# The offsets' outer tap columns moved by two SBUF transfers instead of two shifting products, in a deformable convolution stage

## The reference, cut to what matters

```
x = x + deform_conv(ln_c(x))        # layer 0, the stage that the change is in
    # offset  = conv3x3(ln_c(x), w_off)          18 numbers for each pixel
    # sampled = bilinear gather of ln_c(x) at 9 taps moved by the offsets
    # out     = sum over taps and channels of sampled * w_conv
t = t + top2_experts(ln_t(t))       # layer 0, experts
x = x + fourier_mix(ln_c(x))        # layer 1
t = t + routed_ffn(ln_t(t))         # layer 1
```

## Time and profile before

| | |
|---|---|
| median of 3 runs | 3994.7 us (3988.97 to 3998.19) |
| span of the profiled execution, first to last instruction | 3990.2 us |
| PE busy | 3781.9 us, 95% of the span |
| DVE busy | 2579.8 us, 65% |
| ACT busy | 1794.4 us, 45% |
| POOL busy | 1553.5 us, 39% |
| queue q1 (SP's transfers) | 630.17 MB, 57.1% of 16 engines |
| queue q10 (ACT's transfers) | 71.85 MB, 5.8% of 16 engines |

### The profile page before, as it was taken

How to read it: one execution, slowest core, us unless ns; L and a number is a source line. 1 busy time by engine, 2 the same in 40 slices (tenths; PEclk the granted TensorE clock), 3 DMA queues, 4 the chain that set the end, 5 groups by cost and what they waited for, 6 DMA issues and landing times. The chain is left out here.

```text
span 3990.2 us, 88376 instructions
## 1 busy us (share of the span) xinstructions
PE 3781.9 (95%) x31447; PEld 2461.4 (62%) x31447; DVE 2579.8 (65%) x8511; ACT 1794.4 (45%) x4685; POOL 1553.5 (39%) x2661
## 2 busy tenths in 40 slices
PE   6999999999999999999997999999999999997468
PEld 5666666666666666666663566666666666664245
DVE  4444444444444444444426999999999999996633
ACT  4555555555555555555530334344343434344124
POOL 4544545455444544445422333232323233333210
PEclk8999999999999999999997999999999999998755
DMA  6555555555555554555525777777777777885779
GB/s 117 102 97 96 91 93 95 89 101 93 88 97 91 101 92 89 95 91 91 88 47 194 270 276 268 276 269 277 266 278 271 275 271 270 280 300 175 270 292 394
DMA packets 611673, 709.79 MB, mean 178 GB/s; under 512 B 62256, under 2 KB 494256, under 8 KB 594848
## 3 DMA queue, kind: packets, MB, share of 16 engines
q1 hardware_dynamic: 505760, 630.17, 57.1%
q10 hardware_dynamic: 104448, 71.85, 5.8%
q0 software_dynamic: 1024, 2.10, 0.1%
HBM read 521.20 MB, written 181.63 MB: 176 GB/s over the span
## 5 line engine op out<-in xcount | busy, mean ns | idle before, releaser
L366 PE MATMUL a_ob<-a_sr,wcv 128*128 128x512 f32 (+3 forms) x2820 | 1081.6, 518 | 0.8 <-DVE a_xo L496 0.8
L436 ACT COPY a_sr<-a_sb 128x576 f32<-128x576 f32 (+7 forms) x1296 | 621.2, 562 | 903.9 <-PE a_sb L351 895.9
L351 PEld LDWEIGHTS a_sb<-a_tt,a_win 32*128 32x128 f32 x19008 | 655.7, 185 | 264.6 <-issue 247.7
L351 PE MATMUL a_sb<-a_tt,a_win 32*128 32x144 f32 x19008 | 748.6, 300 | 19.2 <-ACT a_sr L436 12.7
L521 POOL TENSOR_TENSOR a_sx<-a_hh 128x576 f32<-128x576 f32 x260 | 377.8, 1453 | 929.9 <-DVE a_hh L473 921.8
L366 PEld LDWEIGHTS a_ob<-a_sr,wcv 128*128 128x128 f32 x2820 | 491.3, 191 | 279.0 <-issue 231.5
L1116 DVE TENSOR_TENSOR b_P<-b_P,b_x 128x1024 f32<-128x1024 f32 x512 | 620.2, 1212 | 1.8 <-DMA b_P<-pd 1.8
L473 DVE TENSOR_SCALAR a_hh<-a_hh 128x576 f32<-128x576 f32 (+1 forms) x128 | 59.5, 465 | 841.0 <-ACT a_hh L415 841.0
L1019 PE MATMUL b_z<-b_P,b_ew 128*128 128x512 f32 x1024 | 463.4, 595 | 0.0
L1022 PE MATMUL b_z<-b_P,b_ew 128*128 128x512 f32 x1024 | 460.3, 592 | 0.0
L1245 POOL TENSOR_TENSOR b_ss<-b_st 128x12 f32<-128x12 f32 (+2 forms) x139 | 30.0, 216 | 1058.1 <-DVE b_pp L1190 963.8
(11 more groups left out here) (186 smaller groups left out, 5302.4 us busy)
## 6 DMA issues: line engine op xcount, KB each, us to landing
b_P<-pd SPq DMA_DIRECT2D x128, 2048.0 KB, 7.6
a_win<-xtp SPq DMA_DIRECT2D x2144, 36.0 KB
a_xin<-in_x SPq DMA_DIRECT2D x128, 256.0 KB, 6.3
xtp<-a_tn ACTq DMA_DIRECT2D x128, 256.0 KB, 2.3
x1d<-a_xo SPq DMA_DIRECT2D x128, 256.0 KB, 5.9
b_x<-x1d SPq DMA_DIRECT2D x128, 256.0 KB, 7.5
x2d<-b_xa SPq DMA_DIRECT2D x128, 256.0 KB, 3.4
pw<-x3d SPq DMA_DIRECT2D x128, 256.0 KB, 6.6
```

What stands on the lines that cost most here:

```text
L351: t = e.matmul(d[:, 0:3 * m_, :, NU_ * i:NU_ * i + NU_], win[32 * q:32 * q + 32, half_of(Q, j) % NWH, NWIN // 3 * h + i, :], m, start=(j = ...
L366: t = e.matmul(ob[:, r:r + m, :], k["wcv"][:, 3 * (2 - kr) + kx, :], rows[:, :, t_, :], start=(t_ == 0 and r == 0), stop=(t_ == 8))
L436: a = e.copy(bass.AP(d.tensor, d.offset, [list(d.ap[0]), [1152, ni], [1536, nk], [32, 4], [1, m]]), bass.AP(v.tensor, v.offset, [list(v.ap ...
```

## The change

The two shifting products and their constant go. In their place SP issues two transfers for each group, from `zz` to a new buffer `zs` in SBUF: column kx = 0 from partitions 0..126 to 1..127, column kx = 2 from 1..127 to 0..126, 72 numbers (288 bytes) for each partition. `zs` is set to zero once, so the edge rows stay zero. `zz` is laid out with the tap column ahead of the row, so that a column is contiguous. DVE adds three operands in two instructions, the second waiting on the first. The PE wait of `conv` half 1 on `on_ready` goes, since the PSUM bank is no longer shared. In the table `offs` moves from slot 2 to 4, `offs_out` from 3 to 5, `reach` from 4 to 5, `place` from 3 to 4, `hats` from 4 to 5 and `bend` from 7 to 8.

```diff
@@ order_a
             put(t0 - 1, "zsum", Z)
             put(t0 + 1, "shift", Z)
-            put(t0 + 2, "offs", Z)
-            put(t0 + 3, "offs_out", Z)
-            put(t0 + 4, "reach", Z)
-            put(t0 + 3, "place", Z)
-            put(t0 + 4, "hats", Z)
-            put(t0 + 7, "bend", Z)
+            put(t0 + 4, "offs", Z)
+            put(t0 + 5, "offs_out", Z)
+            put(t0 + 5, "reach", Z)
+            put(t0 + 4, "place", Z)
+            put(t0 + 5, "hats", Z)
+            put(t0 + 8, "bend", Z)
             put(t0 + 9, "clip", Z)
@@ phase_a, buffers
-    zz = S("a_zz", [128, 2, 4, 3, 18])
+    zz = S("a_zz", [128, 2, 3, 4, 18])
+    zs = S("a_zs", [128, 2, 2, 4, 18])
@@ phase_a, tensor
-                if h:
-
-                    w.wait_ge(on_ready, min(G - 2, NG - 1) + 1)
-            elif o[0] == "shift":
-                G = o[1]
-                w.wait_ge(z_step, z_count[G])
-
-                w.wait_ge(on_ready, G)
-                w.wait_ge(y_ready, 4 * min(G + 2, NG))
-
-                for kx in (0, 2):
-                    t = e.matmul(OF[:, :, :], k["shift"][:, kx, :], zz[:, G % 2, :, kx, :], start=(kx == 0),
-                                 stop=(kx == 2))
-                t.then_inc(shifted, 1)
@@ phase_a, vector
-                w.wait_ge(shifted, G + 1)
+                w.wait_ge(shifted[G % 2], 32 * (G // 2 + 1))
+                w.wait_ge(z_step, z_count[G])
...
-                e.tensor_tensor(on[:, G % 2, :, :], OF[:, :, :], zz[:, G % 2, :, 1, :], ALU.add).then_inc(on_ready, 1)
+                e.tensor_tensor(on[:, G % 2, :, :], zs[:, G % 2, 0, :, :], zz[:, G % 2, 1, :, :], ALU.add
+                                ).then_inc(on_half, 1)
+                w.wait_ge(on_half, G + 1)
+                e.tensor_tensor(on[:, G % 2, :, :], on[:, G % 2, :, :], zs[:, G % 2, 1, :, :], ALU.add
+                                ).then_inc(on_ready, 1)
@@ phase_a, sync
+            elif o[0] == "shift":
+                G = o[1]
+                w.wait_ge(z_step, z_count[G])
+                w.wait_ge(filled, 1)
+                w.wait_ge(on_ready, G - 1)
+                e.dma_start(zs[1:128, G % 2, 0, :, :], zz[0:127, G % 2, 0, :, :]).then_inc(shifted[G % 2], 16)
+                e.dma_start(zs[0:127, G % 2, 1, :, :], zz[1:128, G % 2, 2, :, :]).then_inc(shifted[G % 2], 16)
```

More of the change, by code:

```diff
@@ L74, in _ @@
             e.dma_start(k["ident"][:, :], ins["ident"][:, :]).then_inc(loaded, 16)
-            e.dma_start(k["shift"][:, :, :], ins["shift"][:, :, :]).then_inc(loaded, 16)
             e.dma_start(k["wcv"][:, :, :], ins["wcv"][:, :, :]).then_inc(loaded, 16)
@@ L78, in _ @@
             e.dma_start(k["cy"][:, :, :], ins["cy"][:, :, :]).then_inc(loaded, 16)
-            e.wait_ge(loaded, 80)
+            e.wait_ge(loaded, 64)
             e.wait_ge(w_in, 16)
@@ L259, in phase_a @@
     YB = [P("a_yb0", [128, 2, 162]), YO[:, 0:324].rearrange("p (r f) -> p r f", r=2)]
-    OF = YO[:, 324:396].rearrange("p (r f) -> p r f", r=4)
     SB = P("a_sb", [128, 4, 512])
@@ L268, in sem @@
         return sems[-1]
-    turned, convolved, shifted, sampled, conv_out = (
-        sem(n) for n in ("turned", "convolved", "shifted", "sampled", "conv_out"))
+    turned, convolved, sampled, conv_out = (
+        sem(n) for n in ("turned", "convolved", "sampled", "conv_out"))
+    shifted = [sem(f"shifted{i}") for i in range(2)]
     normed, y_ready, bent, sr_ready = (sem(n) for n in ("normed", "y_ready", "bent", "sr_ready"))
+    on_half = sem("on_half")
     filled, bn_done, mv_ready, on_ready, reached, clipped, weighed_dve, turned_s, x1_ready = (
@@ L443, in vector @@
         e.memset(sx[:, :, :, :], 0.0)
+        e.memset(zs[:, :, :, :, :], 0.0)
         e.memset(tt[:, :, 2304:2306], 0.0).then_inc(filled, 1)
@@ L527, in gpsimd @@
                 q = G % GI
-                v = yr[:, 4 * G % NYR * 162:(4 * G % NYR + 4) * 162].rearrange("p (r k f) -> p r k f", r=4, k=3)
-                z = zz[:, G % 2, :, :, :].rearrange("p r k f -> p r (k f)")
+                v = yr[:, 4 * G % NYR * 162:(4 * G % NYR + 4) * 162].rearrange("p (r k x f) -> p r k x f", r=4, k=3, x=3)
+                z = zz[:, G % 2, :, :, :].rearrange("p x r f -> p r x f")
                 n = z_count[G]
@@ L1711, in program @@
             SA = lambda name, shape, dt=F32: ca.enter_context(nc.sbuf_tensor(name, shape, dt))
-            k |= {"zero": SA("zero", [128, 640]), "wof": SA("wof", [128, 162]), "shift": SA("shift", [128, 3, 128]), "wcv": SA("wcv", [128, 9, 128]),
+            k |= {"zero": SA("zero", [128, 640]), "wof": SA("wof", [128, 162]), "wcv": SA("wcv", [128, 9, 128]),
                   "cx": SA("cx", [128, 9, NI]), "cy": SA("cy", [128, 14, NJ])}
@@ L1734, in constants @@
     ident = np.eye(128, dtype=np.float32)
[L1735 to L1738, removed]
     x, t, i = np.arange(128)[:, None, None], np.arange(9)[None, :, None], np.arange(NI)[None, None, :]
@@ L1754, in constants @@
     rev = np.ascontiguousarray(ident[:, (128 - np.arange(128)) % 128])
-    return {"io": io, "rev": rev, "ident": ident, "shift": shift, "cx": np.ascontiguousarray(cx), "cy": np.ascontiguousarray(cy), "base": base, "far": far}
+    return {"io": io, "rev": rev, "ident": ident, "cx": np.ascontiguousarray(cx), "cy": np.ascontiguousarray(cy), "base": base, "far": far}
 OUTN = ["out"]
```

## The result

The changed kernel takes 4417.07 us (median of 4 runs, 4415.35 to 4429.97) against 3991.84 us for the kernel before on the same chip (4 runs), a ratio of 1.106 with a 95% interval of 1.104 to 1.108. The forecast was 4585 us with a range of 4420 to 4980: the loop that it named is there, and the loss is 425 us instead of 590, just under the low end of the range.

A forecast was written before the change was run, and what follows sets the result against it. PE bound the deformable stage before; after the change a loop of 2.5 + 11.5 + 5.6 + 1.0 = 20.6 us a step would. 3990 + 580 (120 steps) + 20 (image ends) - 5 (PE's waits) = 4585 us, range 4420 to 4980.

The forecast's parts named there:

- The closed loop: Deformable stage: `xtp` issue, windows, shift, offsets, `offd`, next `xtp` bound the step at 20.6 us instead of 15.75.
- One engine for 127 rows: Shift transfers: 127 is prime, so one DMA engine carries 254 packets in a row for the two shifts.
- Term 3, the shifts' own data: In the loop: 254 packets at 22 ns on one engine, 5.6 us (4.6 at 18 ns, 14 at 55).
- my lower bound of 18 ns: Shift packets' least cost, taken from an `offd` packet, also 288 B from SBUF.
- The other terms of the loop: `xtp` issue to first window 2.5 us, first window to `x1d` landing 11.5, shift landing to next `xtp` issue 1.0.
- The landing of `offd`: `offd` takes 5.8 us to land while the windows' data lag, against a fixed cost of about 2.0.
- The ends of images: At the end of three images SP issues 32 windows before a shift: about 7 us each, 20 us.
- The start: Start-up: zeroing `zs` and the dropped constant cost nothing, since other loads hide them.
- The 5 us of PE's waits: PE's waits on POOL in the deformable stage, 4.8 us, would go and were subtracted in the sum.
- The chain of `bend`: `bend` 2.05 us later moves PE's first final product to 915.01 from 914.53, costing 0.48 us a step without the loop.
- the sign: In the profile after, PE's idle time lies ahead of sample h = 2 or h = 0, released by ACT's copies.
- PE's clock: Deformable stage: PE 74% busy may lose clock; it decides only below a mean of 0.74; within the forecast.

The follow-up runs named there:

- e4: Changed kernel with ACT issuing `offd` behind `xtp`, in slot 9 instead of 5, 127-row shifts kept: 4237.38 us, ratio 1.06 to the kernel before.
- e2: Changed kernel with only the shift of column kx = 0 issued and column kx = 2 left out of the offsets: 4158.79 us, ratio 1.0404.
- e3: Changed kernel with both shifts moving only two of a group's four rows, 144 bytes a packet instead of 288: 4222.57 us, ratio 1.0563.
- e1: Changed kernel with each shift cut into a transfer of 112 rows and one of 15: 4141.25 us, ratio 1.0365.
- e9: e8 with the first four window sets one per step ahead of the shifts, and an image end's second set two slots later: 4005.86 us, ratio 1.0017.
- e7: Changed kernel with shifts cut into 112 + 15 rows and `offd` issued in slot 9; `bend` stays in slot 8: 4050.88 us, ratio 1.0135.
- e8: e7 with `bend` back in slot 7: 4026.2 us, ratio 1.0065.
- e6: Kernel before without its two shifting products, with `bend` moved from slot 7 to 8: 3987.57 us, ratio 0.996.

## Why the prediction was right in its mechanism and wrong in its size

**The closed loop: right.** `xtp` waited behind `offd`, `offd` behind the offsets and the offsets for the shifts in nearly every step, as counted above, and opening the loop at `offd` (e4) takes 44% of the loss away. Half the packets (e2), half the bytes (e3) and more engines (e1) shorten the step too, so the shifts' data lie on the loop.

**One engine for 127 rows: right,** shown by the packet count of the changed kernel and by e1.

**Term 3, the shifts' own data: mis-sized, the step that failed.** The prediction said "I take 22 ns, between the first two. 254 x 22 ns = 5.6 us (4.6 at 18, 14 at 55)". It measured 3.9 us from the first to the last of the 254 packets in one buffer (15.6 ns each) and 4.5 us in the other (18.0 ns), 4.2 in the mean. The mean from first window to the columns is 15.5 us where 11.5 + 5.6 = 17.1 was summed. The rest of that difference is smaller: the first packet of a shift moves 10.7 us after the first window, 0.9 before `x1d` has landed, and DVE starts 0.6 us after the last one; the prediction had the shifts start when `x1d` lands, and nothing behind their last packet. I had divided busy time by packets and taken it for the time between packets, but the packets on this engine overlap: 7.8% of 16 engines over 132 packets is 18.9 ns busy each, at a spacing of 15.2. That also made my lower bound of 18 ns no bound. 1.6 us over 120 steps are 190 us, more than the whole miss of 168. That the result came to within 3 us of the range is owed in part to errors at the ends and the start that went the other way.

**The other terms of the loop: right.** 2.5, 11.5 and 1.0 us were forecast. In the changed kernel `x1d` lands 11.5 us after the first window in the mean, and the other two are 2.38 and 1.00.

**The landing of `offd`.** The prediction held 5.8 us against a fixed cost of about 2.0 from the Trainium skill, page "DMA: Bandwidth & Descriptors", section "Anatomy of one DMA". That section is about transfers that GpSimd issues, and the shifts are issued by SP. Nor do the 5.8 us say what a transfer costs by itself: in the changed kernel, where ACT issues `offd` after the windows' data have passed, the same 36 KB land in a median of 1.5 us.

**The ends of images: mis-sized the other way.** I put 7 us on each of three. From the `xtp` issue at 656.06 the next one in the changed kernel is at 691.97:

```profile
656.06 0.45 ACTq L375 DMA_DIRECT2D xtp<-a_tn  x1
...
691.97 0.45 ACTq L375 DMA_DIRECT2D xtp<-a_tn  x1
```

35.9 us against 23.3 before, 12.6 more; the other two ends have 13.5 and 11.9 more. 32 windows lie ahead of the shift, 12.36 us of issue alone, and their data as well.

**The start: missed.** "At nothing: other loads hide them" held for the constant and the zeroing, but the shifts themselves were overlooked: SP's list has those of the first two groups ahead of the first window, and the second waits for the second group's sums. The windows start at 40.38 us instead of 20.48, and PE, which waits for them, samples first at 54.30 instead of 41.27, 13 us later.

```profile
54.30 3.26 PE L338 MATMUL a_sb<-a_tt,a_win 32*128 32x144 f32 x48 [12.66 <-DMA a_win<-xtp]
```

e9 shows that the windows alone are not the cause: with them ahead the shifts are late instead.

**Where the whole difference lies.** The spans of the profiled executions, cut at the `xtp` issues and taken against the kernel before (3990.2 us; it ran up to 10 us longer on the other chips):

| us more than before | after | e1 | e4 | e7 | e8 | e9 |
|---|---|---|---|---|---|---|
| start, up to the 7th `xtp` issue | 28.7 | 19.8 | 18.3 | 14.8 | 20.9 | 14.2 |
| 112 steps inside the images | 345.1 | 78.8 | 169.0 | -1.4 | -20.3 | -20.4 |
| ends of three images, three steps each | 55.3 | 37.2 | 41.8 | 32.4 | 34.0 | 16.6 |
| behind the last `xtp` issue | 8.8 | 5.7 | 10.4 | 9.1 | 7.8 | 6.2 |
| whole span | 437.9 | 141.5 | 239.5 | 54.8 | 42.3 | 16.6 |

The forecast sum put 580 us on 120 steps, 20 on the ends and nothing on the start. The steps inside the images took 3.08 us more each, 370 for 120, so the steps alone were put 210 us too high, over the whole miss of 168; the ends and the start, both put too low, made up for part of it. The 5 us of PE's waits are no term of their own, since they are part of a step of before. The profiled execution of the changed kernel is its slowest of four, 4430 us, 13 over the median.

**The chain of `bend`: right in place, too big in size** (0.31 us a step in e6 for 0.48). In the changed kernel it costs nothing, as said, though it is seen: PE's longest wait there is the one for DVE's residual ahead of the final products (226.9 us in all, 122 times), and the one for ACT's copies ahead of the samples, which the prediction named as the sign, comes to 134.2. PE is not on the loop, so neither sets the step.

**PE's clock: no part of the bound, as far as is seen.** The granted clock fell to 0.92 in the stretch above, from 1.00 before and above the 0.74 at which the prediction would have had it decide.

The forecasts of e1, e7 and e8 missed mostly where the table says: in e7 and e8 all of the loss stands at the start, at the ends of the images and behind the last step, which I had put at some 6 us an end or left out. In e1 79 of 142 us stand in the steps. There I had taken the landing of the columns for a fixed time; from step to step it varies by 0.6 us (standard deviation), and a loop with little slack pays each late one without getting the early ones back. That this makes up e1's part in the steps, beside the later last issue, is argued, not tested by itself.

## What to carry to other kernels

Before moving work from a busy engine to a transfer, follow the transfer's place in its queue: what stands ahead of it, what waits for its result, and whether that result gates an entry which in turn gates the transfers ahead. Such a loop bounds the step even where every engine is idle a seventh of the time. Here moving one entry of an issue list took 44% of the loss away and cutting the transfers two thirds; both together left nothing of it in the steps. What stays are the places where the pattern breaks, the start and the ends of the images: sum them by themselves. Count the engines of a transfer by its small packets, and cut a prime number of rows (127) into pieces that divide well. To price packets in a row, read the spacing of such packets, not their busy time.

## What the runs showed that I had not expected

The same shift costs by its buffer. The two halves of `zz` and `zs` alternate from group to group, and so does the packets' spacing: 131 packets in 2 us in one group and 108 in the next, 15.3 and 18.5 ns in these stretches, in the DMA view of the changed kernel from 1026.5 to 1028.5 us and from 1045 to 1047 us.

```profile
DMA packets 131, 0.04 MB, mean 19 GB/s; under 512 B 131, under 2 KB 131, under 8 KB 131
```

```profile
DMA packets 108, 0.03 MB, mean 15 GB/s; under 512 B 108, under 2 KB 108, under 8 KB 108
```

Over all groups between 400 and 1700 us the 254 packets take 3.9 us in the one and 4.5 in the other. In e3, with 144 B for each packet, both take 2.7 us. So the buffer matters at 288 B and not at 144 B; what in the two places makes the difference is open.

The issue of the second shift holds SP up: its issue takes 0.6 us at the least and 4.1 in the median (minimum, median and maximum in ns), while the first takes 0.62. The load of x behind it is issued later by that much; nothing in the chain of waits shows that this costs time. Why the issue takes so long is open.

```profile
L602 SPq DMA_DIRECT2D a_zs<-a_zz x128: 613/619/1020, 23.8 to 2465.5; - x128
L603 SPq DMA_DIRECT2D a_zs<-a_zz x128: 603/4131/7849, 24.6 to 2466.2; - x128
```
